# Splitting the sums of squares: k's norm by one wide square on ScalarE and a reduction on VectorE

## The reference, cut to what matters

```
q = (hs @ q_w.T + q_b).reshape(B, L, nh, d)
k = (hs @ k_w.T + k_b).reshape(B, L, nh, d)
v = (hs @ v_w.T + v_b).reshape(B, L, nh, d)
beta = softplus(hs @ b_w.T + b_b)
qn, kn = l2norm(q / scale), l2norm(k / scale)      # over the 128 of one head
attn = einsum('bnhid,bnhjd->bnhij', qn, kn)         # within chunks of 64
out = einsum('bnhij,bnhjd->bnhid', attn * mask, beta * v)
out = (out * silu(hs @ og_w.T)) @ o_w.T + o_b
```

## Time and profile before

| | |
|---|---|
| median of three runs | 2280.7 us (2278.02 to 2284.63) |
| the profiled execution's own time | 2280.73 us |
| its span in the trace | 2279.0 us |
| TensorE busy | 2198.6 us, 96% of the span |
| VectorE busy | 1177.8 us, 52% |
| ScalarE busy | 1031.1 us, 45% |
| GpSimd busy | 537.5 us, 24% |
| granted TensorE clock, mean | 0.99 |

### The profile page before, as it was taken

One profiled execution on the slowest core, in us unless ns is written; L12 is line 12 of the kernel. 1 busy time (PEld: TensorE's weight loads), 2 busy tenths in 40 slices (PEclk: granted clock), 3 DMA queues, 4 the chain that ended last, 5 costly groups with the idle time before them and its releaser, 6 DMA issues.

```text
span 2279.0 us, 34067 instructions
## 1 busy us (share of the span) xinstructions
PE 2198.6 (96%) x11436; PEld 1848.0 (81%) x11436; DVE 1177.8 (52%) x2171; ACT 1031.1 (45%) x3276; POOL 537.5 (24%) x543
## 2 busy tenths in 40 slices
PE   7899899999999999999999999999999999999998
PEld 6788788888878888878888888788878888888887
DVE  4455455555555654555554444555555545545554
ACT  4555545545555555555555454233432333333332
POOL 2244334333333343434343434000000000000000
PEclk8999999999999999999999999999999999999999
DMA  8453541553543534513323230252334223423221
GB/s 280 155 175 127 177 134 35 155 150 111 146 133 90 167 109 156 159 48 108 122 71 114 89 120 29 84 190 97 116 120 162 98 98 103 162 96 116 97 97 61
DMA packets 192780, 276.50 MB, mean 121 GB/s; under 512 B 99184, under 2 KB 132960, under 8 KB 192608
## 3 DMA queue, kind: packets, MB, share of 16 engines
q1 hardware_dynamic: 192608, 274.33, 37.7%
HBM read 214.79 MB, written 59.51 MB: 120 GB/s over the span
## 4 chain that ended last, share of the span: by engine, by line
PE 52%; DVE 1%; ACT 1%; issue 1%; DVEq 0%; ACTq 0%
PE proj_ps L635 26%; PE out_ps L635 8%; PE s_ps L911 3%; PE av_ps L911 3%; PE kt_ps L911 3%; PE qt_ps L911 3%; PE av_ps L842 2%; PE s_ps L833 1%; PE qt_ps L819 1%; PE kt_ps L824 1%; PE misc_ps L714 0%; PE misc_ps L658 0%; PE misc_ps L681 0%; ACT squares L1039 0%; PE misc_ps L649 0%
## 5 line engine op out<-in xcount | busy, mean ns | idle before, releaser
L635 PE MATMUL proj_ps<-w_qkv,h_t 128*128 128x512 f32 x2304 | 616.9, 406 | 7.5 <-PE misc_ps L701 0.9
L635 PEld LDWEIGHTS proj_ps<-w_qkv,h_t 128*128 128x128 f32 x2304 | 414.3, 191 | 93.8 <-issue 18.1
L635 PE MATMUL proj_ps<-h_t,w_qkv 128*128 128x512 f32 x1800 | 443.3, 391 | 0.9 <-DVE acc L1357 0.9
L591 POOL TENSOR_TENSOR inv_norm<-guarded,minus_half 128x8 f32<-128x8 f32 x128 | 209.4, 1636 | 803.3 <-DVE guarded L1329 803.3
L635 PEld LDWEIGHTS proj_ps<-h_t,w_qkv 128*128 128x128 f32 x1800 | 336.0, 188 | 71.5 <-issue 2.8
L1030 ACT ACTIVATE q_t<-qt_ps 128x512 f32<-128x512 f32 x128 | 76.3, 596 | 337.9 <-PE qt_ps L819 337.9
L635 PE MATMUL proj_ps<-h_t,w_gate 128*128 128x512 f32 x768 | 195.8, 407 | 18.7 <-ACT gate L1053 16.7
L1316 DVE TENSOR_TENSOR q_sb<-proj_ps,bias 128x512 f32<-128x512 f32 x128 | 88.3, 690 | 219.8 <-PE proj_ps L635 206.8
L635 PEld LDWEIGHTS proj_ps<-h_t,w_gate 128*128 128x128 f32 x768 | 143.8, 193 | 57.8 <-ACT gate L1053 25.7
L1039 ACT ACTIVATE squares<-q_sb 128x128 f32<-128x128 f32 x512 | 151.4, 298 | 51.3 <-DVE q_sb L1316 46.8
L1316 DVE TENSOR_TENSOR v_sb<-proj_ps,bias 128x512 f32<-128x512 f32 x128 | 88.5, 691 | 154.6 <-PE av_ps L842 154.4
(11 more groups left out here) (184 smaller groups left out, 3298.8 us busy)
## 6 DMA issues: line engine op xcount, KB each, us to landing
w_qkv<-tile_scr SPq DMA_DIRECT2D x100, 768.0 KB, 4.3
w_qkv<-head_scr SPq DMA_DIRECT2D x45, 1024.0 KB, 11.3
head_scr<-stage SPq DMA_DIRECT2D x30, 512.0 KB, 3.0
w_gate<-head_scr SPq DMA_DIRECT2D x15, 1024.0 KB, 5.0
w_out<-head_scr SPq DMA_DIRECT2D x15, 1024.0 KB, 6.3
tile_scr<-stage SPq DMA_DIRECT2D x25, 512.0 KB, 3.4
x_in<-_attn_hidden_states_dram SPq DMA_DIRECT2D x16, 512.0 KB, 5.6
h_scr<-stage SPq DMA_DIRECT2D x16, 512.0 KB, 3.2
```

Source lines behind the costliest of these rows:

```text
L591: pool.tensor_tensor(inv_norm[b][:, :], guarded[b][:, :], minus_half[:, :], ALU.pow).then_inc(inverted, 1)
L635: mm = pe.matmul(out, w, y, start=(j == 0 and m == 0), stop=(3 * j + m == n - 1))
```

## The change

Q's four squares stay as they are: four activations of 128 x 128, each of which also gives one head's sum. K's four become one activation of 128 x 512 without a sum, and VectorE gets a reduction of 128 x 512 to 128 x 4 just ahead of the guard. VectorE waits for its own reduction by a new semaphore (`summed`) before the guard reads it. ScalarE's square of k waits until the reduction of the pass before has read the buffer.

```
-        q_squared, k_squared, guard_done, inverted = (sem("q_squared"), sem("k_squared"),
+        q_squared, k_squared, summed, guard_done, inverted = (sem("q_squared"), sem("k_squared"), sem("summed"),
                                                               sem("guard_done"), sem("inverted"))
...
             def square(n, what):
                 act.wait_ge(biased[what], n + 1)
+                if what == K:
+                    after(act, summed, n)
+                    act.activation(squares[:, K, :], raw[K][n % 2][:, :], ACT.Square).then_inc(k_squared, 1)
+                    return
                 after(act, guard_done, n - 1)
                 for h in range(HG):
                     at = slice(h * P, (h + 1) * P)
-                    m = act.activation(squares[:, what, at], raw[what][n % 2][:, at], ACT.Square,
-                                       accum_out=sumsq[n % 2][:, what * HG + h:what * HG + h + 1])
-                m.then_inc((q_squared, k_squared)[what], 1)
+                    m = act.activation(squares[:, Q, at], raw[Q][n % 2][:, at], ACT.Square,
+                                       accum_out=sumsq[n % 2][:, h:h + 1])
+                m.then_inc(q_squared, 1)
...
             def sum_squares(n):
+                dve.wait_ge(k_squared, n + 1)
+                after(dve, guard_done, n - 1)
+                dve.tensor_reduce(sumsq[n % 2][:, HG:2 * HG], heads(squares[:, K, :]), AX.X, ALU.add).then_inc(summed, 1)
+                dve.wait_ge(summed, n + 1)
                 dve.wait_ge(q_squared, n + 1)
-                dve.wait_ge(k_squared, n + 1)
                 after(dve, inverted, n - 1)
                 dve.tensor_scalar(guarded[n % 2][:, :], sumsq[n % 2][:, :], NORM_EPS2, None, ALU.max).then_inc(guard_done, 1)
```

## The result

The changed kernel takes 2295.56 us in the median of six runs (2293.62 to 2301.43), the kernel before 2279.78 in the median of six beside it. The ratio is 1.0067, with an interval of 1.0056 to 1.0078: 15 us slower (15.8 by the medians, 15.3 by the ratio). The profiled execution took 2297.84 us. In what follows "pass 51" always means pass n = 51 of the loop. (Where the text ahead says "scores of pass n-1" for `score`, `attend`, `mask` and `apply_gate`, that is the code's own count from one; the data are those of the pass two before. No step hangs on it.)

The account below looks back on a forecast made before the run. TensorE, busy 96%, bounds the kernel, so only its waits or slower clock count. Uncovered delays of 15.9 us plus 4.8 us for clock falls make 20.7, on 2280.7 giving 2301 us; range 2287 to 2311.

Parts of the forecast that it names:

- the head of the chain: Where the reduction is put: guard, v's bias, `apply_gate`, `hi_part`, SiLU or copy, then TensorE; delay 0.72 us.
- The operations: K's new square on ScalarE 0.63 us, the reduction on VectorE 0.68 us, about 0.04 us more for the guard's wait.
- ScalarE's relief costs and brings nothing: ScalarE ends its squares about 0.65 us sooner, but the gain goes into waiting for TensorE and VectorE; costed at nothing.
- even: Passes where the guard waited for ScalarE's squares: path from k's first square to guard 1.39 us against 1.36.
- Gates: Third gate projection at t = 1 needs the first SiLU, behind `hi_part`; nine passes of 0.70, 6.3 us.
- Layer norm's transposes: Second half of the transposes waits for ScalarE's read of the first; passes 19, 51, 83 at 0.72, 2.2 us.
- Spread: TensorE's `spread` follows ScalarE's copy of routing weights; passes 36, 44, 68, 76, 100 and 108, together 3.6 us.
- rstd: Queued behind GpSimd's chain, which the guard starts; VectorE waits for it in passes 25, 57, 89; 3 x 0.72 = 2.2 us.
- Passes 4 and 60: Pass 4, a weight transpose waits, 0.7 us; pass 60, q's bias follows v's without a gap, mask late, 0.3 us.
- The eight small ones: Some eight waits behind passes with 0.65 us of cover, 0.08 us each, 0.6 us in all.
- The other late passes reach nothing: Delay in passes 1, 24, 28, 43, 75, 92 costs nothing: K(n+1) has 0.9 us to spare, or no task waits.
- The clock: Longer TensorE waits in passes 4, 19, 51, 83, 25 bring three falls to 1.2 GHz, 1.6 us each, 4.8 us.

Follow-up runs that it names:

- late_passes_only: Against the kernel before: k's wide square and its reduction in 32 passes where v's bias had little or no cover; 2295.43 us, ratio 1.0059.
- covered_passes_only: Against the kernel before: k's wide square and its reduction in the other 96 passes, 32 passes left as before; 2278.26 us, ratio 0.9987.
- reduction_only: Against the changed kernel: k's four accumulating squares restored, the reduction kept into a tile nobody reads; 2320.73 us, 1.0168 of the kernel before.
- act_side_only: Against the changed kernel: wide square of k kept, reduction removed, guard takes q's sums for k; 2275.61 us, 0.9972 of the kernel before.

## Why the prediction was right

The forecast of 2301 was 5 us above the measured 2295.6, which lies in the range, and the mechanism is the one that late_passes_only and covered_passes_only show: a delay at the head of the chain, paid where nothing covers it. By its steps:

- *The operations.* 0.63 and 0.68 us were taken; 0.628 and 0.683 were measured. The guard follows 0.04 us behind the reduction. The Trainium skill's table ("VectorE: DVE Perf Modes", "The perf-mode tier table"), by which the operation has the one-element mode alone, agrees with 683 ns for 512 elements, beside 691 for the two-operand bias. That it is the slowest VectorE operation, as the Trainium skill's rules for authors on that page say, does not hold here, where the bias takes 691 ns and `gated_lo` 970, part of that beside GpSimd.
- *ScalarE's relief costs and brings nothing.* Right for the change as a whole. Its idle time ahead of the copy of q grew by 71 us. But "even" hides two parts, as reduction_only shows, and alone the relief is worth 5 us of waits (act_side_only).
- *Gates*: 6.3 us were taken. The nine passes lost 0.61 to 0.86 each, 6.1 together.
- *Layer norm's transposes*: 2.2 taken; 0.65, 0.67 and 0.66 in passes 19, 51 and 83.
- *Spread*: 3.6 taken, 2.8 found. 100 and 108 lost half of what was set for them.
- *rstd*: 2.2 taken; 0.56, 0.71 and 0.69 around passes 24, 56 and 88.
- *Passes 4 and 60*: 0.7 and 0.3 taken, 0.69 and 0.61 found. The eight small ones don't show.
- *"The other late passes reach nothing"* is the term of waits that was mis-sized. Passes 43 and 75 lost 0.69 each, 28 and 92 0.44 and 0.41, and of those with a little cover 35 and 67 lost 0.99 and 0.67, 99 and 107 0.42 and 0.41: 4.7 us. The delay reached TensorE through the mask, since VectorE ran without a gap from v's bias to the mask of the next pass: in pass 36 `attend` waits 0.41 us for it, where it did not wait before. Together the losing passes made 18.8 us, not 15.9; less the 1.6 that came back in the passes behind, which the sum left out, 17.2.
- *The clock* is the step that failed in its sign: three more falls, 4.8 us, were forecast, from waits that pass 1.6 us. The trace of before already spoke against such a rule. Behind the passes TensorE waits 2.22 us and the clock stays at 1.00:

```profile
1428.12 0.70 PE L635 MATMUL out_ps<-gated_hi,w_out 128*128 128x512 f32 x2 [2.22 <-ACT gated_hi L1047]
```
```profile
1428.00:1430.00 2.00, 1.88 (x8) 1.00 0.00 0
1430.00:1432.00 2.00, 1.12 (x6) 1.00 0.00 0
```

After, behind waits of 1.62 (pass 51) and even 2.07 us (pass 4) it didn't fall either. TensorE in pass 4 of the changed kernel and the stretches behind it (us, busy us, granted clock):

```profile
95.52 0.66 PE L689 MATMUL misc_ps<-ident,nat 128*128 128x128 f32 x4 [2.07 <-DVEq L1244]
```
```profile
95.00:97.00 2.00, 1.33 (x7) 1.00 0.35 139
97.00:99.00 2.00, 2.00 (x15) 1.00 0.94 249
```

And two falls that the trace of before had, in passes 40 and 72, were not there, and in 53 and 85 the clock was low for half as long. Without the 0.28 us a wait of passes 40 and 72 this gave 5 us back in the passes, and the mean clocks of all the executions, 0.992 against 0.990, say the same. So what was measured is 17 us of waits by the steps, some 20 by the estimate over all executions, less 5 for the clock, where 15.9 and 4.8 more were forecast. The two errors, waits too few and the clock's wrong sign, partly cancel: that 2301 came so near is in part luck, and a place-by-place sum stands on firmer ground than the number of falls taken from one execution.

The signs named in advance came as told but one: ScalarE's busy time down 81.6 us (80), VectorE's up 93.5 (87; `gated_lo` ran 10 us longer against GpSimd), gate waits 22.9 in 21 (25, more than 16), L951 5.2 (5.3), v's bias idle 42 us less (40). The one that did not come is more stretches with the clock at 0.50: there were fewer.

## What to carry to other kernels

When work moves from one idle engine to another, its price is not the busy share but what stands behind it in the new engine's order: find the passes in which the next critical instruction follows without a gap, and follow each delay to the engine that bounds. Where cover differs from pass to pass, apply the edit only where there is cover; here this turned +0.7% into -0.1%, and with eight guards moved into -0.7%, about half of the last being the clock. A move that shortens one chain lengthens every queue behind the moved instruction, GpSimd's too, so try it everywhere once, read the gains and losses by place, and keep the gains. Before comparing two times, part each into span x clock and the rest: over the executions of the kernel before the first has a standard deviation of 1.3 to 1.6 us, the span itself 2.4 to 2.9, and it tells waits from falls of the clock.

## What the hardware showed that was not expected

- A wait of TensorE of 1.61 us in passes 40 and 72 was followed by a fall to the 0.50 clock in the traces of two kernels and by none in those of two others. A wait of 2.07 us passed without a fall in the changed kernel, one of 2.22 in the kernel before, and one of 1.07 us in reduction_only was followed by one. The runs of the kernel before spread over 2276.6 to 2286.3 us, with mean clocks of 0.992 at the fast end and 0.987 at the slow one.
- A VectorE operation on four elements a partition, L1119, took 0.45 us beside GpSimd's scaling and 0.17 us clear of it; the long one ended at 485.39, the scaling at 485.36. The reduction ahead of the guard starts GpSimd's chain 0.7 us later against VectorE's, which was enough to part them.
